# Expert down products of two tiles issued together, their 64-row remainders on the two row halves of TensorE's array

## The chip, the cores and the metric

The kernel runs on one core of a Trainium2 chip. Its engines are TensorE (PE; its weight loads are shown apart as PEld), VectorE (DVE), ScalarE (ACT), GpSimd (POOL) and SyncE (SP), which work at the same time and are ordered only by semaphores. The metric is the device time of one execution in microseconds (us); less is better. Before the change the median of three runs is 740.0 us (739.35 to 742.32).

## The reference

1024 tokens of width 256 pass through two layers, each an attention block and a mixture of experts, each with layer norms around it and a residual. Only the routed experts matter here. Cut to them:

```python
# layer 0: every token goes to its top 4 of 32 experts, inner width I = 192
g = silu(einsum('th,eih->tei', xf, gate_w)); u = einsum('th,eih->tei', xf, up_w)
routed = einsum('tei,ehi,te->th', g * u, down_w, combine)
# layer 1: the same with inner width F = 176 and at most 128 tokens for an expert
g = einsum('ech,ehf->ecf', buf, w_gate); u = einsum('ech,ehf->ecf', buf, w_up)
y = einsum('ecf,efh->ech', silu(g) * u, w_down)
```

All of this is in fp32.

## The kernel before

The routed work is sorted by expert and cut into tiles of at most 128 rows: 63 in layer 0 (`NTILE[0]`; the last of them may be empty, which depends on the routing) and 32 in layer 1. Tiles have a running number `g` over both layers (`E0` is 0 and 63) and a number `i` in their layer. A tile goes through these stages:

- **SP** loads the expert's weights, 512 KB into a ring of eight slots (`w_ex`) and the last 64 rows of the down weights into `w_rest`, where an even `g` takes partitions 0 to 63 and an odd one partitions 64 to 127. A slot is loaded again when `e_down` says that the tile eight before is done (lines 634 to 649).
- **POOL** gathers 128 token rows with an indirect DMA (layer 0 has 32 such row tiles, layer 1 has 32), and later scatters a tile's result rows to DRAM (`rows_to_outs`, line 812, in order of tiles).
- **PE, ups** (`e_up`, line 1185): gate and up products. The inner width of 192 (176) is 128 plus a remainder of 64; so there are three 128-column blocks by two halves of the contraction, 6 matmuls of 128x128 by 128 columns. An fp32 matmul is two weight loads and two matmuls in the trace, so they are 12 entries of line 1196. Rows are turned by PE ahead of that (`e_transpose`, line 1167), one row tile a step until all 32 are turned (after step 28).
- **ACT** (`e_silu`, lines 1486 and 1488) and **DVE** (`e_mult`, lines 2102 and 2106): silu and product. The remainder's product goes to the 64 rows of `eact` that belong to the parity of `g`; the other 64 rows are zeros that POOL wrote once per layer (line 800).
- **PE, down** (`e_down`, line 1201): 128 rows of the inner width by 256 columns (line 1209), then the remainder (line 1211) with all 128 rows of `w_rest`, half of which meets the zeros. Each is two entries of the trace. The result stands in PSUM bank 6 or 7, by the parity of `g`.
- **DVE** (`e_out`, line 2109) copies the bank to SBUF. Before a down may write its bank, PE waits for `e_sb` to reach `g - 1` (line 1206): the tile two before, in the same bank, has been copied out.

The order on PE is written out: step `i` gives out the transposes, the ups of tile `i`, and then the down of tile `i - 3` (`LAG` is 3, line 1242). The order on DVE is written out as well and is not touched by the change: step `i` is `e_mult(i)` and then `e_out(i - 3)` (line 2117). ACT's is `e_tile` (copy of turned rows) and `e_silu(i)`.

Behind the loop, the four choices of each token are summed from DRAM: SP loads four planes of 1 MB each (line 673), DVE adds them (line 2137). In layer 0 the loads wait until every tile that has rows is written; in layer 1 plane `k` waits for the tiles up to `28 + k`. In layer 1 PE has four products of the shared expert to do behind the loop (line 1132).

Elsewhere in the kernel PE uses a part of the array: in attention `weigh` (line 1014) issues four fp32 matmuls with 32 weight columns each, one for each quarter of the columns of the array; lines 1143 and 1175 use 32 of its rows.

Of the kernel before, what the change touches and what calls it, by code (L numbers as in the profile page):

```python
# [14 lines left out]
P = 128  # L15
T = 1024
NT = T // P
D = 256
KD = D // P
# [33 lines left out]
HALF = P // 2  # L53
FULL = 1
SFULL = tuple(w // P for w in SHARED)
UPC = 2 * FULL + 1
EW = KD * UPC * P + D
# [3 lines left out]
NTILE = (NROWT + E - 1, E)  # L61
E0 = (0, NTILE[0])
NR = (E, E + 1)
RING = 4
ROW_RING = 8
# [3 lines left out]
LAG = RING - 1  # L69
# [22 lines left out]
def turn_before(i):  # L92

    return min(2 * i + 1, i + LAG)


def copy_before(i):

    return min(2 * i + 1, i + LAG)


GATES_AT = D
# [192 lines left out]
def build(nc, a, out):  # L295
    ctx = ExitStack()
    with ctx:
        sems = {}

        def S(name):  # L300
            if name not in sems:
                sems[name] = ctx.enter_context(nc.semaphore(name))
            return sems[name]
# [120 lines left out]
        eact = X[:, 2048:3072].rearrange("p (r n) -> p r n", r=RING)  # L424
# [9 lines left out]
        w_ex = KAf[:, 0:ROW_RING * EW].rearrange("p (r n) -> p r n", r=ROW_RING)  # L434
        w_rest = X[:, 6144:6144 + ROW_RING // 2 * D].rearrange("p (r n) -> p r n", r=ROW_RING // 2)
# [69 lines left out]
        ps = ctx.enter_context(nc.psum_tensor("ps", [P, 8, CH], F32))  # L505
# [177 lines left out]
        def _(pool):  # L683
# [58 lines left out]
            for L in range(2):  # L742
# [52 lines left out]
                    pool.wait_ge(S("zero_rest"), 1)  # L795
                pool.memset(acts[L][HALF:P, f * T:(f + 1) * T], 0.0).then_inc(S("zero_rest"), 1)
                pool.memset(w_sdn[HALF:P, f, :], 0.0).then_inc(S("zero_rest"), 1)
                for x in range(2):
                    no = HALF * (1 - x)
                    pool.memset(eact[no:no + HALF, x::2, P:2 * P], 0.0).then_inc(S("zero_rest"), 1)  # L800

                def rows_in(i):
                    g = NROWT * L + i
# [53 lines left out]
        def _(pe):  # L857
# [19 lines left out]
            for L in range(2):  # L877
# [21 lines left out]
                for i in range(NT):  # L899
                    pe.wait_ge(S(f"qk_sb{L}"), i // 2 + 1)  # L900
                    dst = ps[:, qk_bank(L, i // 2), i % 2 * D:(i % 2 + 1) * D]
                    for k in range(KD):
                        mm = pe.matmul(dst, xT[:, k, i * P:(i + 1) * P], w_qkv[:, 2, k, :],
                                       start=(k == 0), stop=(k == KD - 1))
# [132 lines left out]
                def shared_up(u, those=(0, 1), ks=range(KD)):  # L1037
                    n, j = divmod(u, nsc)
                    q = UP_POS[L][u]
                    if L == 1 and q >= 2:  # L1040
                        pe.wait_ge(S(f"s_act{L}"), q - 1)
                    those = those if j < SFULL[L] else those[:1]
                    for x in those:
                        col = (x * SFULL[L] + j if j < SFULL[L] else 2 * SFULL[L]) * P
                        for k in ks:
                            mm = pe.matmul(ps[:, up_bank(L, u, x), :], w_sgu[:, k, col:col + P],  # L1046
                                           xT[:, k, n * CH:(n + 1) * CH], start=(k == 0), stop=(k == KD - 1))
                    if (those[-1] == 1 or j == SFULL[L]) and ks[-1] == KD - 1:
                        mm.then_inc(S("s_gu"), 1)
# [30 lines left out]
                if L == 0:  # L1080

                    for j in range(NT):
                        mm = pe.matmul(ps[0:E, LISTS, 0:1], picked[:, j, :], ones[:, 0:1], start=(j == 0), stop=(j == NT - 1))
                    mm.then_inc(S("counts"), 1)

                for i in range(NT):
                    for j in range(i + 1):
                        mm = pe.matmul(ps[:, RANKS, i * E:(i + 1) * E], (ones if j < i else before)[:, :],
                                       picked[:, j, :], start=(j == 0), stop=(j == i))
                mm.then_inc(S(f"ranks{L}"), 1)  # L1090
                if L == 0:
# [9 lines left out]
                    for x in range(2):  # L1101
                        mm = pe.matmul(ps[0:E, LISTS, 2 * E + 1 + x:2 * E + 2 + x], upto_n[:, E * x:E * (x + 1)], ones[0:E, 0:1],
                                       start=True, stop=True)
# [3 lines left out]
                def list_tokens(quarters):  # L1107

                    wide = 2 * NROWT
                    parts = token_parts  # L1110
                    for q in quarters:
                        pe.wait_ge(S("token_hi"), NT * L + QT * (q + 1))
                        if L == 1 or q < QUARTERS - 1:
                            pe.wait_ge(S("token_lo"), (QUARTERS - 1) * L + q + 1)
                        pe.wait_ge(S("at_place"), QUARTERS * L + q + 1)
                        for i in range(QT * q, QT * (q + 1)):
                            for k in range(K):
                                mm = pe.matmul(ps[:, LISTS, 2 * P:2 * P + wide], at_place[:, i, k, :],
                                               parts[:, i, k, :, :].rearrange("p a n -> p (a n)"),
                                               start=(i == 0 and k == 0), stop=(i == NT - 1 and k == K - 1))  # L1120
                    if quarters[-1] == QUARTERS - 1:
                        mm.then_inc(S("token_ps"), 1)
# [3 lines left out]
                def shared_down(i):  # L1126
                    pe.wait_ge(S(f"s_act{L}"), nsc * (i // TPC + 1))
                    banks = (SHARED_EARLY, 2)[L]
                    if i >= banks:
                        pe.wait_ge(S("sh_sb"), NT * L + i - banks + 1)  # L1130
                    for j in range(nsc):
                        mm = pe.matmul(ps[:, shared_bank(L, i), 0:D], actv[:, j, i * P:(i + 1) * P], w_sdn[:, j, :],  # L1132
                                       start=(j == 0), stop=(j == nsc - 1))
                    mm.then_inc(S("sh_down"), 1)

                if L == 0:
                    pe.wait_ge(S("zero_rest"), 1 + 4)
                    for i in range(SHARED_EARLY):
                        shared_down(i)
                    list_tokens((0,))  # L1140
                    pe.wait_ge(S("seg_of"), 1)
                    pe.wait_ge(S("dest_done"), 1)
                    pe.matmul(ps[:, RANKS, 0:4 * TILES[0]], ones_f[0:E, :], seg_of.rearrange("p a n -> p (a n)"),
                              start=True, stop=True).then_inc(S("seg_ps"), 1)
                    list_tokens((1, 2, 3))
                    for i in range(SHARED_EARLY, NT):
                        shared_down(i)
                else:
                    for u in UP_ORDER[1][nsc:]:
                        shared_up(u)  # L1150
                        if u == LIST_AFTER:
                            list_tokens(range(QUARTERS))
                    pe.wait_ge(S("zero_rest"), 1 + 4 * 2)
                    for i in range(TPC):
                        if i < 2:
                            pe.wait_ge(S("s_act1"), nsc * NC - 2 + 2 * i)
                        shared_down(i)
# [40 lines left out]
                                           start=(k == 0), stop=(k == KD - 1))  # L1198
                    mm.then_inc(S("e_up"), 1)

                def e_down(i):
                    g = E0[L] + i
                    r = g % ROW_RING
                    pe.wait_ge(S("e_act"), 2 * g + 2)
                    if g >= 2:
                        pe.wait_ge(S("e_sb"), g - 1)
                    if g == 1:
                        pe.wait_ge(S("places"), 1)
                    pe.matmul(ps[:, 6 + g % 2, 0:D], eact[:, g % RING, 0:P], w_ex[:, r, KD * UPC * P:EW],  # L1209
                              start=True, stop=False)  # L1210
                    mm = pe.matmul(ps[:, 6 + g % 2, 0:D], eact[:, g % RING, P:2 * P], w_rest[:, r // 2, :],  # L1211
                                   start=False, stop=True)
                    mm.then_inc(S("e_down"), 1)

                pe.wait_ge(S("dest_done"), L + 1)
                pe.wait_ge(S(f"s_act{L}"), nsc * NC)
# [4 lines left out]
                def load_place(i):  # L1221

                    if L == 0 and i < NTILE[0]:
                        places_of[i] = pe.value_load(seg_at[0:1, i:i + 1], min_val=0, max_val=(NROWT - 1) * P)
# [3 lines left out]
                for i in range(NTILE[L] + LAG):  # L1228
                    if i < NTILE[L]:
                        load_place(i + 1)  # L1230
                        while turned_to <= min(turn_before(i), NROWT - 1):
                            e_transpose(turned_to)
                            turned_to += 1
                        if L == 0 and i == 2:
                            pe.wait_ge(S("sh_sb"), NT)
                        e_up(i)
                    if L == 0 and i < 2:
                        (turn_list, spread_list)[i]()
                    if L == 1 and i == LAG:
                        pe.wait_ge(S("sh_sb"), NT + TPC)  # L1240
                    if i >= LAG:
                        e_down(i - LAG)
                for i in range(TPC if L == 1 else NT, NT):
                    shared_down(i)
                if L == 0:
# [2 lines left out]
                for k in range(K):  # L1248
                    pe.wait_ge(S("gate_diag"), K * len(ON_PE[0]) * L + len(ON_PE[L]) * (k + 1))
                    for x, i in enumerate(ON_PE[L]):  # L1250
                        if x == 0 or k == K - 1:
                            pe.wait_ge(S(f"sum_in_{k}_{i // TPC if k == K - 1 else 0}"), 16 * (L + 1))
                        mm = pe.matmul(ps[:, 2 + x, 0:D], gate_diag(L, x, k), sums[L][k][:, i, :],
                                       start=(k == 0 and L == 1), stop=(k == K - 1))
# [1032 lines left out]
```

## Time and profile before

| | us |
|---|---|
| median of three runs | 740.0 |
| the profiled execution | 741.1 |
| its span from the first to the last instruction | 739.4 |
| PE matmul busy | 661.2 (89%) |
| PE weight load busy | 429.0 (58%) |
| DVE busy | 479.0 (65%) |
| ACT busy | 327.0 (44%) |
| POOL busy | 265.2 (36%) |
| expert loop of layer 0, first ups to last copy out | 221.0 to 373.4 |
| expert loop of layer 1 | 630.1 to 708.3 |

Busy shares are means over stages with different limits, so the rows below are taken from the two expert loops and what follows each. A PE matmul's entry starts when it is issued to the array and its end is modelled; the time from one start to the next is what tells the rate.

### The profile page before, as it was taken

To read this page: it belongs to the slowest core of one execution; us is meant where nothing else is said; L and a number is where in the kernel's file an instruction comes from. 1 tells how busy PE (TensorE), PEld (TensorE's weight loads), DVE (VectorE), ACT (ScalarE), POOL (GpSimd) and SP (SyncE) were. 2 spreads that over 40 slices of the span, in tenths; PEclk is the share of its full clock that TensorE was granted. 3 is DMA by queue.
4 is the path that set the end of the run, shared out by engine and by line. 5 is a ranking of instruction groups with operands and counts; after the bars stand their busy time and mean duration, and the time that the engine had idled before them with its cause. 6 is when DMAs were issued, how large, how long until landed. Compare 5 with 4: busy or idle time off the path is not lost. (4 is left out here: it accounts for less than half of the span.)

```text
span 739.4 us, 13365 instructions
## 1 busy us (share of the span) xinstructions
PE 661.2 (89%) x4292; PEld 429.0 (58%) x4292; DVE 479.0 (65%) x1357; ACT 327.0 (44%) x686; POOL 265.2 (36%) x313
## 2 busy tenths in 40 slices
PE   4988999998779999999966887999998999999991
PEld 3633343335358999999953523343344446999980
DVE  3688888864663446445476798888865685344457
ACT  3554666673153333224412443666664230433322
POOL 4150212111266776444431282112111203677631
PEclk9998999999799999999996989999999999999995
DMA  3534210070049999999670444011000710489762
GB/s 103 171 115 130 66 37 1 1 233 25 30 133 308 311 334 301 299 311 309 223 256 1 129 136 136 16 52 71 1 2 1 257 53 25 155 284 316 238 215 92
DMA packets 60295, 108.60 MB, mean 147 GB/s; under 512 B 11194, under 2 KB 37131, under 8 KB 60100
## 3 DMA queue, kind: packets, MB, share of 16 engines
q1 hardware_dynamic: 52532, 93.86, 39.0%
q0 software_dynamic: 7632, 13.86, 5.6%
q8 instruction: 36, 0.59, 0.3%
q14 instruction: 31, 0.25, 0.1%
q10 hardware_dynamic: 64, 0.03, 0.0%
HBM read 79.98 MB, written 19.79 MB: 135 GB/s over the span
## 5 line engine op out<-in xcount | busy, mean ns | idle before, releaser
L1364 ACT ACTIVATE X<-ps 128x1024 f32<-128x1024 f32 (+1 forms) x192 | 147.5, 810 | 81.9 <-PE ps L1000 81.3
L1690 DVE TENSOR_REDUCE mx<-ps 128x1 f32<-128x512 f32 (+3 forms) x208 | 129.5, 674 | 26.2 <-PE ps L932 17.1
L932 PE MATMUL ps<-KA,QA 112*128 112x512 bf16 (+3 forms) x384 | 117.8, 343 | 7.9 <-DVE mx L1690 3.3
L815 POOL DMA_INDIRECT outs<-w_sgu,token x95 | 95.4, 1004 | 74.7 <-DVE w_sgu L2115 59.6
L779 POOL TENSOR_SCALAR_AFFINE_SELECT X<-X 128x512 f32<-128x512 f32 x64 | 40.7, 637 | 203.7 <-ACT X L1364 203.7
L2102 DVE TENSOR_TENSOR X<-ps,X 128x128 f32<-128x128 f32 x95 | 27.6, 291 | 113.3 <-ACT X L1488 111.7
L1000 PE MATMUL ps<-QA,KA 114*128 114x512 bf16 (+3 forms) x384 | 95.6, 332 | 2.4 <-ACT X L1364 1.2
L1196 PE MATMUL ps<-QA,KA 128*128 x756 | 96.1, 277 | 0.8 <-issue 0.8
L1196 PEld LDWEIGHTS ps<-QA,KA 128*128 128x128 f32 x756 | 92.9, 193 | 3.6 <-issue 1.8
L932 PEld LDWEIGHTS ps<-KA,QA 112*128 112x128 bf16 x384 | 37.1, 98 | 86.2 <-DVE mx L1690 41.3
L807 POOL DMA_INDIRECT V<-token_rows,row_of_slot x64 | 65.6, 1025 | 53.8 <-DVE row_of_slot L2010 31.5
L1014 PE MATMUL ps<-X,V 128*32 128x512 f32 (+3 forms) x768 | 81.5, 500 | 0.6 <-POOL X L779 0.6
L1486 ACT ACTIVATE X<-ps 128x128 f32<-128x128 f32 x95 | 26.3, 277 | 109.0 <-PE ps L1196 108.0
L1687 DVE CUSTOM_DVE_ANT_0 xT<-ps,xT 128x384 bf16<-128x384 f32 (+1 forms) x96 | 56.7, 620 | 8.1 <-PE ps L932 7.1
L1046 PE MATMUL ps<-xT,w_sgu 128*128 128x512 f32 x112 | 55.0, 635 | 3.7 <-POOL rstd L731 2.2
L1000 PEld LDWEIGHTS ps<-QA,KA 114*128 114x128 bf16 x384 | 33.6, 99 | 41.5 <-ACT X L1364 16.5
L1209 PE MATMUL ps<-KA,X 128*128 128x256 f32 x190 | 56.9, 381 | 0.3
L1211 PE MATMUL ps<-X 128*128 128x256 f32 x190 | 56.5, 379 | 0.0
L1196 PE MATMUL ps<-X,KA 128*128 128x128 f32 x384 | 48.2, 275 | 0.3 <-ACT X L1477 0.3
L1196 PEld LDWEIGHTS ps<-X,KA 128*128 128x128 f32 x384 | 45.6, 192 | 0.6 <-ACT X L1477 0.5
L2115 DVE COPY w_sgu<-ps 128x256 f32<-128x256 f32 x95 | 40.3, 424 | 4.2 <-PE ps L1211 1.2
L1211 PEld LDWEIGHTS ps<-X 128*128 128x128 f32 x190 | 36.1, 190 | 4.9
(319 smaller groups left out, 891.0 us busy)
## 6 DMA issues: line engine op xcount, KB each, us to landing
KA<-in_ex SPq DMA_DIRECT2D x95, 512.0 KB
X<-in_dn SPq DMA_DIRECT2D x95, 64.0 KB
outs<-empty SPq DMA_DIRECT2D x4, 1024.0 KB, 8.0
V<-outs SPq DMA_DIRECT2D x4, 1024.0 KB, 6.1
QA<-X SPq DMA_DIRECT2D x28, 128.0 KB, 2.5
KA<-X SPq DMA_DIRECT2D x28, 128.0 KB, 2.6
QA<-w_sdn SPq DMA_DIRECT2D x28, 128.0 KB, 2.5
KA<-parts_k SPq DMA_DIRECT2D x28, 128.0 KB, 2.5
```

The costliest lines, as they stand in the source:

```text
L807: pool.indirect_dma_start(out=rows[:, g % ROW_RING, :], out_offset=None, in_=token_rows[L], in_offset=bass.IndirectOffsetOnAxis(ap=row_of_ ...
L815: pool.indirect_dma_start(out=outs[L], out_offset=bass.IndirectOffsetOnAxis(ap=token[L][:, i:i + 1], axis=0), in_=erows[:, g % OUT_RING, : ...
L932: mm = pe.matmul(ps[:, bank, j * w:(j + 1) * w], QA[0:KQ, h, i * P:(i + 1) * P], KA[0:KQ, h, s0:s0 + w], start=True, stop=not diag or mask ...
L1000: mm = pe.matmul(ps[:, 4 + 2 * p + x, off:CH], KA[0:KX, h, b * P:(b + 1) * P], QA[0:KX, h, c * CH + off:(c + 1) * CH], start=True, stop=True)
L1014: mm = pe.matmul(ps[32 * x:32 * x + 32, RB, off:CH], V[:, b, HG * g + x, :], probs[:, st % PB, x, off:CH], start=(b == 0), stop=(b == TPC ...
L1046: mm = pe.matmul(ps[:, up_bank(L, u, x), :], w_sgu[:, k, col:col + P], xT[:, k, n * CH:(n + 1) * CH], start=(k == 0), stop=(k == KD - 1))
L1196: mm = pe.matmul(ps[:, 2 + g % RING, m * P:(m + 1) * P], w_ex[:, r, col:col + P], rowsT_all[:, k, bass.ds(at, P)] if L == 0 else rowsT(L, ...
L1209: pe.matmul(ps[:, 6 + g % 2, 0:D], eact[:, g % RING, 0:P], w_ex[:, r, KD * UPC * P:EW], start=True, stop=False)
L1211: mm = pe.matmul(ps[:, 6 + g % 2, 0:D], eact[:, g % RING, P:2 * P], w_rest[:, r // 2, :], start=False, stop=True)
L1364: nc.scalar.activation(probs[:, st % PB, 2 * p:2 * p + 2, off:CH], ps[:, 4 + 2 * p:6 + 2 * p, off:CH], ACT.Exp, scale=SCALE).then_inc(S(f" ...
L1687: ins = v.tensor_tensor_reduce(mask_sums[:, u % 2, 0:w], ps[:, n % RB, 0:w], mask_wide[:, CH - w:CH], 1.0, -BIG, ALU.add, ALU.max, mx[:, p ...
L1690: ins = v.tensor_reduce(mx[:, part, i, h0:h0 + nh], ps[:, n % RB, 0:nh * w].rearrange("p (h w) -> p h w", h=nh), AX.X, ALU.max)
```

## The change

A step no longer gives out one down. `downs_after` says after which step which downs come: two at a time behind every second step, an even `g` and the odd one after it, and single ones at the ends (tile 62 of layer 0, tiles 0 and 31 of layer 1). `e_downs` gives out the 128-row parts of the two tiles first and then the two remainders, each with 64 rows of weights and 64 rows of data in place of 128. The zeros aren't written any more.

```diff
+def downs_after(L, i):
+
+    if i < NTILE[L]:
+        return tuple(x for x in (i - 3, i - 2) if x >= 0) if (E0[L] + i) % 2 else ()
+    return {NTILE[L]: (NTILE[L] - 3, NTILE[L] - 2), NTILE[L] + 1: (NTILE[L] - 1,)}.get(i, ())
...
-                for x in range(2):
-                    no = HALF * (1 - x)
-                    pool.memset(eact[no:no + HALF, x::2, P:2 * P], 0.0).then_inc(S("zero_rest"), 1)
...
-                def e_down(i):
-                    g = E0[L] + i
-                    r = g % ROW_RING
-                    pe.wait_ge(S("e_act"), 2 * g + 2)
-                    if g >= 2:
-                        pe.wait_ge(S("e_sb"), g - 1)
-                    if g == 1:
-                        pe.wait_ge(S("places"), 1)
-                    pe.matmul(ps[:, 6 + g % 2, 0:D], eact[:, g % RING, 0:P], w_ex[:, r, KD * UPC * P:EW],
-                              start=True, stop=False)
-                    mm = pe.matmul(ps[:, 6 + g % 2, 0:D], eact[:, g % RING, P:2 * P], w_rest[:, r // 2, :],
-                                   start=False, stop=True)
-                    mm.then_inc(S("e_down"), 1)
+                def e_downs(those):
+                    for i in those:
+                        g = E0[L] + i
+                        pe.wait_ge(S("e_act"), 2 * g + 2)
+                        if g >= 2:
+                            pe.wait_ge(S("e_sb"), g - 1)
+                        if g == 1:
+                            pe.wait_ge(S("places"), 1)
+                        pe.matmul(ps[:, 6 + g % 2, 0:D], eact[:, g % RING, 0:P], w_ex[:, g % ROW_RING, KD * UPC * P:EW],
+                                  start=True, stop=False)
+                    for i in those:
+                        g = E0[L] + i
+                        half = slice(HALF * (g % 2), HALF * (g % 2) + HALF)
+                        pe.matmul(ps[:, 6 + g % 2, 0:D], eact[half, g % RING, P:2 * P], w_rest[half, g % ROW_RING // 2, :],
+                                  start=False, stop=True).then_inc(S("e_down"), 1)
...
-                    if L == 1 and i == LAG:
+                    if L == 1 and i == LAG - 1:
                         pe.wait_ge(S("sh_sb"), NT + TPC)
-                    if i >= LAG:
-                        e_down(i - LAG)
+                    e_downs(downs_after(L, i))
```

The counts that PE waits for on `zero_rest` are lowered by the two writes that are gone.

## Rows read from the trace of the kernel before

**Rows 1.** Stretch of layer 0's loop: us, PE, PEld, DVE, ACT, POOL busy, clock, DMA

```profile
300.99:316.41 15.42, 15.42 (x114) 14.70 (x112) 7.07 (x22) 3.81 (x14) 6.88 (x8) 1.00 0.94 302
```

**Rows 2.** Chain that ended last, loop of layer 1: start, us, what

```profile
664.56 1.34 PE ps L1196 x12
...
666.98 1.34 PE ps L1196 x12
...
700.48 1.34 PE ps L1196 x12
...
702.25 0.43 PE ps L1211 x2
702.68 1.35 PE ps L1196 x12
```

**Rows 3.** Timeline, layer 0, ups of tile 32 and what follows them

```profile
300.99 1.50 PE L1196 MATMUL ps<-QA,KA 128*128 x12
...
302.52 0.28 ACT L1486 ACTIVATE X<-ps 128x128 f32<-128x128 f32 x1 [1.63 <-PE ps L1196]
...
303.12 0.29 DVE L2102 TENSOR_TENSOR X<-ps,X 128x128 f32<-128x128 f32 x1 [1.13 <-ACT X L1488]
...
303.77 0.42 DVE L2115 COPY w_sgu<-ps 128x256 f32<-128x256 f32 x1
```

**Rows 4.** Timeline, layer 0's last ups (tile 62) and the downs behind them

```profile
367.59 1.50 PE L1196 MATMUL ps<-QA,KA 128*128 x12
...
370.38 0.91 DVE L2115 COPY w_sgu<-ps 128x256 f32<-128x256 f32 x2
370.92 0.30 PEld L1209 LDWEIGHTS ps<-KA,X 128*128 128x128 f32 x2 [0.50 <-issue]
...
371.45 0.59 PE L1211 MATMUL ps<-X 128*128 128x256 f32 x2
```

**Rows 5.** Timelines and one line's durations: attention's column-quarter matmuls between full ones

```profile
520.66 0.38 PE L932 MATMUL ps<-KA,QA 112*128 112x512 bf16 x1
520.97 1.07 PE L1014 MATMUL ps<-X,V 128*32 128x512 f32 x8
...
521.96 0.10 PEld L932 LDWEIGHTS ps<-KA,QA 112*128 112x128 bf16 x1 [0.84 <-issue]
...
L1014 PE MATMUL ps<-X,V x8: 592/604/617, 521.0 to 521.4; 128*32 128x512 f32 x8
```

**Rows 6.** Durations ns (min/median/max) of matmuls just behind a switch of array shape

```profile
L1143 PE MATMUL ps<-X x2: 374/426/478, 210.1 to 210.4; 32*128 32x256 f32 x2
...
L1046 PE MATMUL ps<-xT,w_sgu x3: 592/595/697, 567.4 to 568.8; 128*128 128x512 f32 x3
...
L1167 PE MATMUL ps<-identf,V x2: 273/301/329, 222.6 to 222.8; 128*128 128x128 f32 x2
```

**Rows 7.** Timelines, end of layer 0's loop: a scatter, plane load, plane add

```profile
364.97 0.98 POOL L815 DMA_INDIRECT outs<-w_sgu,token  x1 [1.23 <-DVE w_sgu L2115]
...
366.71 0.40 SPq L673 DMA_DIRECT2D V<-outs  x1
...
379.46 1.67 DVE L2137 SCALAR_TENSOR_TENSOR X<-V,xn,X 128x256 f32<-128x256 f32 x4 [1.62 <-DMA V<-outs]
```

**Rows 8.** Timeline, layer 0, DVE's steps 48 and 50

```profile
340.11 0.29 DVE L2102 TENSOR_TENSOR X<-ps,X 128x128 f32<-128x128 f32 x1 [2.35 <-ACT X L1488]
...
343.94 0.19 DVE L1917 TENSOR_REDUCE gsum<-gate 128x8 f32<-128x32 f32 x1
...
344.83 0.42 DVE L2115 COPY w_sgu<-ps 128x256 f32<-128x256 f32 x1
```

**Rows 9.** Chain that ended last, end of layer 1's loop

```profile
707.79 2.12 DMA outs<-w_sgu,token
...
709.95 7.80 DMA X<-outs
```

**Rows 10.** Timeline, POOL's first instruction behind the zeros of layer 0

```profile
201.91 0.17 POOL L825 CAST X<-X 32x1 f32<-32x1 int32 x1 [10.44 <-DVE X L1948]
```

More of the change, by code:

```diff
@@ L1136, in _ @@
                 if L == 0:
-                    pe.wait_ge(S("zero_rest"), 1 + 4)
+                    pe.wait_ge(S("zero_rest"), 1 + 2)
                     for i in range(SHARED_EARLY):
@@ L1152, in _ @@
                             list_tokens(range(QUARTERS))
-                    pe.wait_ge(S("zero_rest"), 1 + 4 * 2)
+                    pe.wait_ge(S("zero_rest"), 1 + 2 * 2)
                     for i in range(TPC):
```

## The prediction

> **What bounds the kernel now.** I read the stretches of the two expert loops first, then the chain of waits, then the timeline. In a stretch of seven steps of layer 0, PE is busy all of its 15.42 us at a granted clock of 1.00 (the 2.4 GHz level), while DVE is busy 7.07 us, POOL 6.88 us and the DMA engines 0.94 of the time [rows 1]. The chain runs over PE alone: ups 1.34 us, down parts 0.43 us each, and the next ups [rows 2]. A step is 2.20 us where nothing is turned (700.48 to 702.68) and 2.42 us where a row tile is (664.56 to 666.98), so transposes are 0.22. PE sets the pace, and the change works on PE.
>
> All times below count from the start U of a tile's ups. Within a step the ups are 1.34, the 128-row part 0.43 and the remainder 0.43. After the ups comes a chain on other engines: silu begins at U+1.53, the product at U+2.13, and DVE's copy of the down three tiles back runs from U+2.78 to U+3.20 [rows 3]. That copy stands behind the product in DVE's order, and the change leaves this order alone.
>
> **Part 1, the remainders.** Before, two tiles' remainders are four passes of 0.215 us, 0.86 in all [rows 2]. If the halves run side by side they are two, 0.43. Whether passes of separate parts of the array do that is not shown for 64 rows. The nearest rows are the column quarters: eight fp32 passes of 512 columns, each 0.43 at the rate of the 128-row part, start from 520.97 to 521.4 and the next full weight load begins at 521.96, 0.99 us later instead of 3.4 [rows 5]. I take side by side, a gain of 0.43 a pair. The other ends are no overlap (gain 0) and overlap of one pass only (0.215).
>
> **Part 2, the switches of shape.** Each pair goes from the full array to halves and back. Going in, 512 bf16 columns that start at 520.66 have streamed by 520.87 (512 at 2.4 GHz), and the first quarter begins at 520.97: 0.10. Coming back, 0.99 less two rounds of 0.43 and the first quarters' own load (617 against 592 ns) leaves 0.10 [rows 5]. In a plain stream the loads are hidden. Behind a switch the first one isn't: a matmul behind quarters takes 697 ns against 592, so 0.105 for 128 fp32 columns; with 32 rows and 128 columns it is 478 against 374, the same; transposes pay 329 against 273, 0.055 [rows 6]. So a pair pays 0.10 + 0.105 going in and 0.10 + 0.105 (0.055 before transposes) coming back: 0.41 or 0.36. Part 1's 0.43 is eaten but for 0.02 or 0.07 us a pair. If the loads of the two halves follow one another, 0.105 more.
>
> The Trainium skill speaks against the change here: "TensorEngine Tiling (Array Packing)", Key Properties, says that a change of tiling mode, and not merely of the tile, drains TensorE. The rows above agree for quarters and for 32 rows with 0.10 us each way; without that rule the sum would be the second rival's.
>
> **Part 3, the wait that comes new.** The second down of a pair needs the bank of the tile two before it. At PE's step i the pair is tiles i-3 and i-2, and DVE copies tile i-4 out in its step i-1, behind the product of tile i-1. That ends 3.20 behind the start U of the ups of tile i-1 [rows 3]. Before, PE had two steps of slack on this. Now only the ups of tile i and one 128-row part lie between: 1.34 + 1.34 + 0.43 puts the second part at U+3.10, or U+3.32 with 0.22 of transposes. The trace of before holds this very wait, at the loop's end, where three downs follow without ups. The copy of tile 59 ends near 370.8, the weight load waits until 370.92, and the remainder starts at 371.45, so the 128-row part streamed from 371.45 - 0.43 = 371.02, which is U+3.43 [rows 4]. So the second part starts at U+3.43: late by 0.33 without transposes, by 0.10 with them. Behind the wait stands all of PE's stream, the remainders and the next ups too.
>
> **A pair of steps.** Without transposes: 3.43, second part until 3.86, switch 0.205, remainders 0.44, switch 0.205: the ups of tile i+1 start at U+4.70, against 4.41 before. **+0.29.** With them: 3.86 + 0.205 + 0.44 + 0.155 + 0.22 = 4.88 against 4.85, **+0.025** with unrounded terms. DVE's work of a pair, twice 1.07 us, fits, and weight slots come free no later than before by more than 0.1 us, so the DMA's 0.94 doesn't become the bound when the period grows.
>
> **Layer 0.** What ends the layer is the load of the planes: SP's load waits until 367.1, for the scatter that POOL issued at 364.97, tile 56's (the seventh from the last; the tiles behind it hold no rows), and at 379.46 DVE waits 1.62 us for a plane [rows 7]. So I sum up to the copy of tile 56. Twelve pairs with transposes (steps 5 to 27) give 0.3, the first pair, which waits for no bank, -0.1, and fifteen without (steps 29 to 57) 15 x 0.29 = 4.4. In step 50 DVE has 0.89 us of gate work ahead of the copy [rows 8]; that goes into the wait of the pair behind step 51: 0.9. At tile 48 ACT takes an exponential in, and DVE waits 2.35 for it where 1.13 is usual [rows 3, 8]; of these 1.2 us I count 0.1, as the downs of a pair that then lie between the ups of tiles 47 and 48 give ACT 4.70 - 1.34 - 2.20 = 1.16 us more. Tile 56 itself is copied 0.6 later within its pair, since its remainder comes behind its partner's 128-row part, the wait and the switch. Sum 6.2. The last copy (tile 62) moves by more, some 8.3, since its three downs now wait for one another; DVE's adds begin behind it, at 381.7 instead of 373.4, but the third plane lands at 379.4 + 6.2 = 385.6, when two adds of 1.67 are done. So **+6.2**.
>
> **Layer 1.** Tile 0 alone pays two switches with nothing to share, 0.35. Twelve pairs with transposes 0.3, the one behind step 28 0.1, the one behind step 30 0.3, and one more down stands ahead of the last ups, 0.87: the ups of tile 31 end 1.9 later. Behind them, tile 28's copy is where it was; tile 29's comes after its partner's wait, and its scatter follows it at U+5.9 instead of U+5.3: 0.6. Plane 1 waits for that scatter [rows 9]. Planes 0 and 1 start 1.9 and 2.5 later; I take **+2.3**. The shared expert's four products on PE start 3.3 later, but their last consumer waits for plane 1 ahead of them.
>
> **Nothing** comes from the zeros: POOL wrote them ahead of 10.44 us in which it waits for DVE [rows 10]. Without that cover it would be a gain of their own length.
>
> **Sum:** 6.2 + 2.3 = 8.5 us. On the profiled execution's 741.1 (span 739.4 and 1.7 around it) that is 749.6; the median of before is 1.1 less, so **748.5**.
>
> **Rivals.**
> *The halves don't share the array in time.* For it: a remainder's two passes are issued one behind the other, so a strict order would overlap only the first tile's second pass with the second tile's first. Against it: the quarters are issued in the same way and took two rounds. Price: 44 pairs on the path, 44 x 0.215 = 9.5, so 758; with no overlap at all 767. With the two loads in series 44 x 0.105 = 4.6: 753. The Trainium skill, "TensorE: Matmul & The Clock Gate", Part 3, has matmuls start and end strictly in program order, which would give the 758; the quarters' 0.99 us speaks against it.
>
> *The halves need no switch* (faster than before). No row shows a 64-row shape. If a half's weights load behind full matmuls, a pair is 3.86 + 0.44 = 4.30 without transposes (-0.11) and 4.52 with them (-0.33). Layer 0: 15 x -0.11, 12 x -0.33, first pair -0.4, gates and tile 48 1.0, tile 56's place 0.4: -4.7. Layer 1: 12 x -0.33, two more pairs -0.4, one down 0.9, its end 0.4: -3.1. That is 732. It decides from a switch price below 0.1 a pair or so, where the bank wait alone is left.
>
> *The bank is free in time.* If the copy came before the product, pairs would be -0.03 and -0.08: layer 0 -1.3, layer 1 +0.5, 739. Against it: DVE's written order and [rows 4].
>
> **How the numbers follow.** Forecast 0.64 (746 to 751); loads in series 0.08 (753); passes in order 0.12 (758, or 767); no switch 0.06 (732); bank in time 0.10 (739). The range leaves out the no-switch case, half of the last and the longest of the serial case: 741 to 759. A measurement of this kernel tells about 0.5% (3.7 us) from no change. Faster by more is the no-switch case, 0.06; within it the bank case, 0.10; the rest, 0.84, is slower.
>
> **What would show it.** In the changed trace: the 64-row matmuls of line 1211's successor start in twos within some 10 ns, the pair 0.43 and not 0.86; the weight load ahead of them begins 0.10 behind the last full column and the one after them too; in each pair a PE gap before the second 128-row part, 0.33 without transposes, ending just behind DVE's copy; ups 4.70 apart over two steps late in layer 0. I am wrong if the two-step period is 4.41 or less there, if line 1209's second part never waits, or if layer 0's planes start less than 4 us later.

## The result and the profile after

The changed kernel takes 751.1 us (median of four runs, 747.6 to 754.4) against 741.0 (739.4 to 742.3): the ratio of the two is 1.0129, 95% interval 1.0102 to 1.0157, so the change is slower, clear of noise, by less than 2%. Ratios here and below come from runs taken side by side, with runs in a slower state left out, and so are not quite the quotient of the medians. The forecast was 748.5 with a range of 741 to 759, and slower. The profiled execution took 753.05 us with a span of 751.3, 11.9 above the 739.4 of before.

In the changed code the ups stand on line 1200, the 128-row parts on 1213, the 64-row remainders on 1218, DVE's copy on 2120, the planes' loads on 680. The first rows are the chain of waits of the changed kernel in layer 0, late, where nothing is turned (start, us, what; they answer [rows 2]).

```profile
361.00 2.88 PE ps L1200 x24
363.88 0.43 PE ps L1213 x2
364.39 0.67 PE ps L1213 x2
365.06 0.63 PE ps L1218 x4
365.69 2.88 PE ps L1200 x24
```

A pair is 4.69 us (361.00 to 365.69) where two steps were 4.41. The first 128-row part has streamed by 364.31, the second ends at 365.06 and so began at 364.63: 0.32 of waiting, for DVE's copy. Four 64-row passes and the switch ahead of them take 0.63. The four start in twos, 7 ns apart within each two, the second two 0.32 us behind the first. The rows are the first two of the pair at 365.06, then all four, with durations and the first and last start:

```profile
L1218 PE MATMUL ps<-X x2: 480/480/480, 365.0 to 365.0; 64*128 64x256 f32 x2
...
L1218 PE MATMUL ps<-X x4: 376/428/480, 365.0 to 365.3; 64*128 64x256 f32 x4
```

In layer 1's chain a pair with transposes is 4.86 us:

```profile
699.94 0.97 PE ps L1213 x4
...
704.80 0.97 PE ps L1213 x4
```

The loop is as forecast. The ends of the two layers are not. The same chain at layer 0's end, then at layer 1's:

```profile
381.05 0.63 PE ps L1218 x2
381.67 1.92 PE ps L1252 x8
383.60 5.63 PE ps L1258 x26
389.25 0.88 DVE stats L2186 x2
...
711.10 1.55 PE ps L1200 x12
...
718.73 12.61 PE ps L1136 x48
```

Where layer 0 ends, PE now runs without a pause from the last remainder through its twenty products for the sum of the planes (lines 1252 and 1258, 40 entries in the trace, of which the chain names 34), and DVE waits for these. Where layer 1 ends, the chain of before ran over a scatter and a plane's load [rows 9]; now it runs over the four products of the shared expert (line 1136), which took 12.61 us. The windows of that stretch show why (PE, PEld, DVE, ACT, POOL busy, clock, DMA):

```profile
712.40:715.40 3.00, 1.58 (x9) 0.86 (x9) 1.01 (x3) 2.36 (x5) 1.19 (x2) 1.00 0.11 44
715.40:718.40 3.00, 2.40 (x8) 1.00 (x4) 1.66 (x5) 1.21 (x5) 1.71 (x3) 0.60 0.11 44
718.40:721.40 3.00, 3.00 (x8) 2.20 (x8) 0.42 (x1) 1.24 (x5) 1.96 (x2) 0.50 0.81 243
```

PE was busy for 1.58 of 3 us, the downs waiting for one another's copies, and then the granted clock stood at 0.50 (the 1.2 GHz level).

So the 11.9 us of span are: 0.9 that lie ahead of the loop (tile 3's ups start at 231.20 instead of 230.29; no down has been given out by then, and the start of the first ups differs by up to 4.8 us between the profiles of this case), 5.8 in layer 0 (the first product of the attention that follows starts 6.7 later, less the 0.9), 0.1 between the layers, 1.8 in layer 1's loop, 3.3 behind its last ups.

### The profile page after: what moved, and what is told of

Same layout as the page of the kernel before. It is cut to its first block, busy times and chain, and to the rows that moved or that the text cites. A ratio compares the mean times of both kernels' runs of the same rounds, so it can differ in the third digit from the quotient of the medians.

```text
span 751.3 us, 13361 instructions
## 1 busy us (share of the span) xinstructions
PE 669.3 (89%) x4292; PEld 406.2 (54%) x4292; DVE 478.4 (64%) x1357; ACT 326.9 (44%) x686; POOL 263.1 (35%) x309
## 4 chain that ended last, share of the span: by engine, by line
PE 72%; DVE 19%; issue 3%; ACT 2%; DMA 2%; POOL 1%; SPq 1%; ACTq 0%; DVEq 0%; POOLq 0%
PE ps L1200 17%; PE ps L1018 9%; PE ps L936 8%; PE ps L1004 7%; PE ps L1213 6%; DVE mx L1695 5%; PE ps L1050 4%; PE ps L1218 4%; PE ps L1136 3%; PE ps L1171 2%; PE ps L891 2%; PE ps L990 1%; DVE xres L1600 1%; PE ps L969 1%; PE ps L907 1%
## 5 line engine op out<-in xcount | busy, mean ns | idle before, releaser
L1200 PEld LDWEIGHTS ps<-QA,KA 128*128 128x128 f32 x756 | 89.0, 194 | 7.1 <-issue 7.0
L811 POOL DMA_INDIRECT V<-token_rows,row_of_slot x64 | 65.6, 1026 | 57.2 <-DVE row_of_slot L2015 32.1
L1050 PE MATMUL ps<-xT,w_sgu 128*128 128x512 f32 x112 | 53.2, 618 | 3.7 <-POOL rstd L738 2.2
L1213 PEld LDWEIGHTS ps<-KA,X 128*128 128x128 f32 x190 | 28.9, 191 | 20.5 <-issue 16.3
L738 POOL TENSOR_TENSOR rstd<-rs_sq,minus_half 128x4 f32<-128x4 f32 (+1 forms) x14 | 13.6, 969 | 63.1 <-DVE rs_sq L1557 63.1
```

What stands on the lines that cost most here:

```text
L811: pool.indirect_dma_start(out=rows[:, g % ROW_RING, :], out_offset=None, in_=token_rows[L], in_offset=bass.IndirectOffsetOnAxis(ap=row_of_ ...
L1200: mm = pe.matmul(ps[:, 2 + g % RING, m * P:(m + 1) * P], w_ex[:, r, col:col + P], rowsT_all[:, k, bass.ds(at, P)] if L == 0 else rowsT(L, ...
```

## The experiments

The times stand against the kernel before as run beside them on the same chip: 741.95 us for the order without the halves, the halves without the order, the copies a step sooner and the whole product at layer 1's end; 742.66 for the copy-first kernel with its loads spread and the groups of four with rows loaded tile by tile, both forms; 741.77 for the other four.

**The order without the halves.** Zeros and full remainders come back, the pairs stay.

```diff
+                for x in range(2):
+                    no = HALF * (1 - x)
+                    pool.memset(eact[no:no + HALF, x::2, P:2 * P], 0.0).then_inc(S("zero_rest"), 1)
...
-                        pe.matmul(ps[:, 6 + g % 2, 0:D], eact[half, g % RING, P:2 * P], w_rest[half, g % ROW_RING // 2, :],
+                        pe.matmul(ps[:, 6 + g % 2, 0:D], eact[:, g % RING, P:2 * P], w_rest[:, g % ROW_RING // 2, :],
```

> The pairs' order alone: the remainders are full 128-row products again, over zeros in the unused half, so nothing shares the array and no shape is switched. Theory (the new wait for the bank costs the time, halves and switches cancel): a pair of steps late in layer 0 is 3.43 + 0.43 + 0.86 = 4.72 us without transposes (changed kernel 4.69, before 4.41) and 3.43 + 0.43 + 0.86 + 0.22 = 4.94 with them (4.87, 4.85); the whole is 0 to 3 us above the changed kernel, 751 to 754. Rival (the switches of shape cost it, not the order): pairs back at 4.41 and 4.85, the whole at 741.

750.3 us (ratio 1.0117, 1.0072 to 1.0162), as the changed kernel. Its chain in layer 0 (its ups on line 1203, remainders on 1220):

```profile
361.43 2.68 PE ps L1203 x24
364.11 0.43 PE ps L1216 x2
...
364.62 0.67 PE ps L1216 x2
365.29 0.86 PE ps L1220 x4
366.16 2.68 PE ps L1203 x24
```

A pair is 4.73, the wait for the bank is there unchanged, the remainders take 0.86 and no switch stands around them (2.68 for 24 ups instead of 2.88). So the order alone costs what the change costs, and halves with their switches give 0.04 a pair.

**The halves without the order.** One down a step as before, its remainder on its half.

```diff
 def downs_after(L, i):
-    if i < NTILE[L]:
-        return tuple(x for x in (i - 3, i - 2) if x >= 0) if (E0[L] + i) % 2 else ()
-    return {NTILE[L]: (NTILE[L] - 3, NTILE[L] - 2), NTILE[L] + 1: (NTILE[L] - 1,)}.get(i, ())
+    return (i - 3,) if i >= 3 else ()
```

> The halves alone: the order of the kernel before, one down in every step, with its 64-row remainder on its half, so that each tile switches into the halves and back and nothing shares the array. Theory (a switch in and out costs 0.41 us, 0.36 ahead of transposes): a step late in layer 0 goes from 2.20 to 2.61 us, one with transposes from 2.42 to 2.78; with some 30 steps of the one kind on the path of layer 0 and 7 in layer 1, and 29 and 25 of the other, 37 x 0.41 + 54 x 0.36 = 35 us more than before, 776. Rival (halves need no drain of the array, the row-tiled products load their weights behind full ones as any other): steps stay at 2.20 and 2.42, the whole at 741. Between them (only the exposed load of 0.105 each way): 2.41 and 2.58, 758.

771.5 us (1.0403, 1.0357 to 1.0449), 29.5 more than before where 35 were expected; that a step costs 0.02 less than priced makes some 2 of the difference; the rest has not been taken apart. Its chain in layer 0:

```profile
363.13 1.53 PE ps L1198 x12
364.67 0.43 PE ps L1211 x2
365.10 0.63 PE ps L1216 x2
365.73 1.53 PE ps L1198 x12
```

A step is 2.60 us instead of 2.20 [rows 2], with transposes 2.77 instead of 2.42: a switch in and out costs 0.39 and 0.35. And two 64-row passes take 0.63 here, as long as the four of two tiles in the changed kernel. The halves run side by side.

**DVE copies a step sooner.** Both tiles of a pair are copied behind the pair, ahead of the next product.

```diff
-                    if i >= LAG:
-                        e_out(i - LAG)
+                    for x in downs_after(L, i):
+                        e_out(x)
```

> The changed kernel, but DVE copies both downs of a pair out right behind the product of the same step, one step sooner, so that the bank is free when the next pair wants it. Theory (the bank wait is the cost): no gap ahead of the second 128-row part, a pair is 2.68 + 0.86 + 0.205 + 0.43 + 0.205 = 4.38 us without transposes and 2.68 + 0.22 + 0.86 + 0.205 + 0.43 + 0.155 = 4.55 to 4.80 with them (before 4.41 and 4.85), the whole is 738 to 742. Rival 1 (PE is late for another reason, the switches or the loads): the gap stays or moves behind the remainders, pairs at 4.69, the whole at 751. Rival 2 (DVE becomes the bound, since the two copies now wait for PE ahead of the next product): gaps ahead of the 128-row parts that end on DVE's product, a pair above 4.5.

736.4 us (0.9930, 0.9904 to 0.9956): faster than the changed kernel by 2% and than the kernel before by 0.7%, which is clear of noise. Its timelines of PE and then of DVE in layer 0:

```profile
303.26 2.94 PE L1200 MATMUL ps<-QA,KA 128*128 x24
306.04 1.03 PE L1213 MATMUL ps<-KA,X 128*128 128x256 f32 x4
307.00 0.70 PE L1218 MATMUL ps<-X 64*128 64x256 f32 x4
307.63 1.60 PE L1200 MATMUL ps<-QA,KA 128*128 x12
...
303.36 0.76 DVE L2120 COPY w_sgu<-ps 128x256 f32<-128x256 f32 x2 [0.27 <-PE ps L1218]
```

The two 128-row parts are one piece, the gap is gone, a pair is 4.37 us. With transposes it is 4.77, and step 51, where the gates had put 0.89 into the wait, is a step as any. One change of order, on an engine that is idle half of the time [rows 1], was worth some 15 us of the changed kernel. So the wait for the bank is the cost: it goes with the copy's place, and it is there without halves.

**Layer 1's end, filled with a whole product.** One of the shared expert's four products moves between the last pair's 128-row parts, one ahead of the last down.

```diff
                                   start=True, stop=False)
+                        if L == 1 and i == NTILE[1] - 3:
+                            shared_down(TPC)
...
+                    if L == 1 and i == NTILE[1] + 1:
+                        shared_down(TPC + 1)
                     e_downs(downs_after(L, i))
...
```

> The changed kernel, with two of the shared expert's four last products of layer 1 moved up between the last downs, where PE waits for DVE's copies. Theory (PE's idle gaps there let the granted clock fall to 0.50 from 716 to 723 us, which stretches the four products from 10.5 to 12.7 us): the clock stays at 1.00 behind the last ups, the last product ends 3 to 4 us sooner and the whole is 1 to 4 us below the changed kernel, 747 to 750. Rival (the end of layer 1 hangs on the scatter of tile 29 and the planes' loads, not on PE): planes land when they did, the whole within 0.5 us of the changed kernel.

752.1 us (1.0167, 1.0117 to 1.0216), no gain: the rival's number, though the planes did not land when they did before. The clock held at 1.00 and the last product's last matmul began at 726.1 instead of 731.0, but the chain went elsewhere:

```profile
717.46 5.47 DMA outs<-w_sgu,token
...
722.95 5.29 DMA X<-outs
```

A product is 2.6 us long where the gap was 1.42, so tile 29's copy came later and its scatter went out at 717.46, behind plane 0's load of 717.03; it took 5.47 us where it took 2.12 before [rows 9], and plane 1's load waits for it (722.95, against 720.79 in the changed kernel, whose last ups are 0.5 later).

**The same, with half a product.** Three of the product's six chunks in the gap, three ahead of the last down.

```diff
+                        if L == 1 and i == NTILE[1] - 3:
+                            shared_down(TPC, (0, 3))
...
+                    if L == 1 and i == NTILE[1] + 1:
+                        shared_down(TPC, (3, nsc))
...
```

> The changed kernel, with the first half of one of the shared expert's products put into PE's wait of 1.4 us between the last pair's 128-row parts, and its second half ahead of the last down, so that neither down moves by more than some 0.2 us. Theory (the clock that fell to 0.50 behind these waits cost 2 to 3 us at the end): the clock stays at 1.00 until the four products are done, these end 4 us sooner than 730.95, the scatter of tile 29 goes out where it did, and from the last ups to the end takes 32 to 33 us in place of 35.4: 748 to 749. Rival (planes and their loads set the end, as they did where a whole product stood between the parts): products sooner, end within 1 us of the changed kernel, 750 to 752.

748.5 us (1.0094, 1.0058 to 1.0131), where the changed kernel took 752.0 on the same chip. Windows and chain of the stretch:

```profile
712.20:715.20 3.00, 3.00 (x15) 1.86 (x13) 1.66 (x5) 1.16 (x4) 1.74 (x2) 1.00 0.11 44
715.20:718.20 3.00, 3.00 (x14) 2.67 (x15) 1.01 (x3) 1.28 (x5) 1.97 (x2) 1.00 0.88 244
...
713.86 3.91 DMA outs<-w_sgu,token
...
717.79 5.45 DMA X<-outs
```

PE has no gap, the clock stays at 1.00, the scatter goes out ahead of plane 0's load (714.37), and the chain runs over scatter and plane again as it did before the change. From the start of the last ups' last matmul to the start of the last output add it is 32.0 us (709.20 to 741.23) instead of 35.4 (712.36 to 747.74), and it was 32.1 before the change: the 3.3 us are back. This run moves work as well as holding the clock, so it doesn't part the two. The pairs with full remainders do, in the main: they have the same first wait of 1.42 us and no work moved, their clock stayed at 1.00, and there it is 32.6 us (711.99 to 744.55), over a scatter and a plane too. So 2.8 of the 3.3 go with the clock; their second wait is shorter, 0.18 instead of 0.60, so up to some 0.4 of that can be the wait itself.

**The changed kernel once more.**

> The changed kernel once more, as a measure of how its end varies. If the fall of the clock at 716 us belongs to the gaps that the change makes there, it is there again, with some 35 us from the last ups to the end; if it is chance, the clock is 1.00 there and the end takes 32 to 33 us, as in the kernels that also have those gaps. 748 to 753.

752.0 us (750.1 to 755.2). Layer 1's end is the same again (35.5 us, clock 0.64 and then 0.50), in both executions of this kernel that were profiled, and in neither of the two whose gaps were filled. So the fall goes with the gaps and is not the chance of one execution, though the pairs with full remainders, with nearly the same waits, did not have it. In this execution the clock also fell at layer 0's end, where it stayed at 1.00 in the first. Its window there and its first eight matmuls of the planes' sum, which took 1.99 us in the other:

```profile
380.00:383.00 3.00, 3.00 (x8) 2.02 (x7) 2.33 (x6) 0.00 (x0) 2.21 (x3) 0.50 1.09 383
...
380.53 3.78 PE L1252 MATMUL ps<-X,identf 128*128 128x256 f32 x8
```

The three last downs of layer 0 wait for one another as well, 1.42 and 0.60 us in both executions. From the last ups of layer 0 to the first of layer 1 it is 2.4 us longer with the fall (263.0 instead of 260.6). A fall that comes in some executions only fits the spread of 747.6 to 755.2 over the changed kernel's eight runs, but which of them had it is not known beyond the two profiled.

**Who releases layer 0's planes.** In the kernel before, SP's eight register loads, which stand between its last weights' load and the planes' loads, are spread over its last eight weights' loads.

```diff
+                    if L == 0 and REGS_AT <= i < REGS_AT + OUT_RING:
+                        x = i - REGS_AT
+                        those.append(sp.value_load(used_rows[0:1, x:x + 1], min_val=16,
+                                                   max_val=16 * uses(NTILE[0] - 1, OUT_RING)))
...
```

> The kernel before, with SP's eight loads of registers (some 0.55 us each) that stand between the last weights' load of layer 0 and the planes' loads spread over its last eight weights' loads. Theory (SP's own queue releases the planes' loads, not a scatter): the first plane's load goes out 3.5 to 4.5 us sooner than 366.71, at 362.2 to 363.2, DVE no longer waits 1.62 us for the third plane, and the layer ends up to 1.5 us sooner: 739 to 741. Rival (the scatter of the seventh tile from the end, which POOL issued at 364.97, releases them): 366.7 as before, the whole unchanged.

741.1 us (0.9981, 0.9961 to 1.0000). SP's timeline and, from 374.26, the chain:

```profile
362.85 0.48 SPq L607 DMA_DIRECT2D X<-in_dn  x1
363.65 0.40 SPq L678 DMA_DIRECT2D V<-outs  x1
...
374.26 0.43 PE ps L1216 x2
374.69 1.73 PE ps L1252 x8
376.42 5.63 PE ps L1258 x26
```

The planes' loads follow the last weights' load by 0.8 us. Against the last ups they go out 4.8 us sooner than before (6.9 ahead of 370.59, where it was 2.1 ahead of 368.82), the layer's last adds come 2.2 us sooner, and the chain then runs over PE's products. The releaser was SP's own queue. The time is at the edge of what can be told from no change.

**The same in the copy-first kernel.**

> The copy-first kernel with SP's eight register loads of layer 0's end spread over the last weights' loads. The kernel before gained 2.2 us from this between its last ups and the last add of layer 0, and 0.7 in the median. Theory (the same wait stands in the copy-first kernel, which ends that layer 13.3 us behind its last ups): 1 to 2 us less than 736.4, 734 to 736. Rival (DVE's last copy sets the start of the adds, as in the changed kernel, where the planes are there by then): 736 to 737.

738.6 us (0.9945, 0.9920 to 0.9969), the copy-first kernel's time within the intervals: the rival's number. Its chain there runs from the last remainder into PE's planes' products, as in the changed kernel:

```profile
371.54 0.63 PE ps L1223 x2
372.17 1.92 PE ps L1257 x8
374.09 5.62 PE ps L1263 x26
```

In the copy-first kernel itself the planes were not all there: DVE waited for the third, as the theory had it.

```profile
374.34 1.67 DVE L2142 SCALAR_TENSOR_TENSOR X<-V,xn,X 128x256 f32<-128x256 f32 x4 [1.06 <-DMA V<-outs]
```

With the loads spread that wait is gone, but the layer's last add starts only 0.3 us sooner behind the last ups (12.6 us, 12.9 before), since PE's products for the planes now end last.

**Groups of four.** One switch for four tiles, behind every fourth tile's ups: two 128-row parts, four remainders, two 128-row parts, their results in the two halves of the two banks. DVE copies all four behind the group.

```diff
+                    for i in firsts:
+                        part(i, True)
                     for i in those:
...
+                        mm = pe.matmul(ps[:, 6 + g % 2, out_at(g)], eact[half, g % RING, P:2 * P],
+                                       w_rest[half, g % ROW_RING // 2, :], start=i in lasts, stop=i in firsts)
...
+                    for i in lasts:
+                        part(i, False).then_inc(S("e_down"), 1)
```

> Groups of four downs behind every fourth tile's ups, in the order: two 128-row parts, four 64-row remainders (two side by side, twice), two 128-row parts; their results in the two halves of the two banks; DVE copies all four out behind the group. One switch into the halves and back then serves four tiles in place of two. Theory (the halves' gain is eaten by the switch, 0.40 us measured without and 0.345 with transposes): four steps are 4 x 1.34 + 4 x 0.43 + 2 x 0.43 + 0.40 = 8.34 us without transposes (two pairs of the copy-first kernel 8.75, before 8.81) and 4 x 1.56 + 1.72 + 0.86 + 0.345 = 9.17 with them (9.53, 9.70); 15 groups in layer 0 and 7 in layer 1 save 15 x 0.38 + 7 x 0.36 = 8 us of the copy-first kernel's 736.4: 728. Rival 1 (the weights' loads become the bound: the DMA engines are busy for 0.94 of 8.81, 8.28 us in four steps, and four slots now come free together): gaps ahead of the ups that end on DMA, four steps at 8.5 to 8.8, 732 to 736. Rival 2 (DVE's four copies behind one another hold up its products): gaps ahead of the group that end on DVE, four steps above 8.8, 737 or more.

757.9 us (1.0203, 1.0140 to 1.0266). The group itself is as priced: from the first part at 312.02 to the next ups at 315.01 it is 2.99 us (1.72 + 0.86 + 0.40 = 2.98). But PE waits ahead of the ups behind which the next group stands; the second row is a window of layer 0's loop:

```profile
310.58 1.60 PE L1213 MATMUL ps<-QA,KA 128*128 x12 [1.55 <-issue]
...
306.03:316.35 10.32, 8.77 (x68) 7.72 (x68) 3.92 (x14) 2.19 (x8) 3.94 (x4) 1.00 0.84 275
```

Four steps take 10.2 us, PE is busy for 0.85 of the time and the DMA engines for 0.84. The profile names no releaser for that wait ("issue"). The first rival fits it, far beyond its price of 8.8: four slots come free in one burst, and the loads of a tile's remainder rows stand behind those of its pair's second tile. The next run tests this.

**Groups of four, remainder rows loaded tile by tile.**

```diff
                     expert_in(g, e)
-                    if g % 2 == 0 and i + 1 < NTILE[L]:
-                        return e
-                    if g % 2 == 1 and i > 0:
-                        rest_in(g - 1, even)
-                    elif i >= ROW_RING:
-                        sp.wait_ge(S("e_down"), g - ROW_RING + 2)
                     rest_in(g, e)
```

> The groups of four, with each tile's 64 remainder rows of down weights loaded right behind its own other weights, in place of both remainders of a pair behind the second tile's (with halves a tile no longer reads its partner's rows, so it need not wait for them). Theory (in the groups of four, four steps took 10.19 us without transposes as PE waits 1.55 us for weights whose loads wait for each other; DMA's work in four steps is 0.82 to 0.85 of 10.19, 8.4 us): the first tile of a burst is there some 2 us sooner, the gap ahead of the ups closes, four steps take 8.4 to 8.8 us, the whole 728 to 738. Rival (four slots that come free together leave the queue empty whatever the order): a gap of over 1 us stays, four steps at 9.5 or more, the whole at 748 or more.

740.1 us (0.9963, 0.9933 to 0.9993). A window of four steps without transposes, and the longest wait that the trace names for PE between the ups of tiles 9 and 53:

```profile
303.37:311.74 8.37, 8.37 (x66) 7.52 (x65) 3.76 (x12) 2.18 (x8) 3.93 (x4) 1.00 0.99 331
...
290.39 0.44 PE L1178 MATMUL ps<-identf,V 128*128 128x128 f32 x2 [1.35 <-DMA V<-token_rows,row_of_slot]
```

The gaps of over 1 us ahead of the ups are gone, so the order of the loads had made them. PE has its 8.37 where the loads keep up, and the DMA engines are at 0.99 there. Other groups lose this again: between the ups of tiles 9 and 53 the loop takes 100.0 us here and 99.95 in the copy-first kernel. The waits that the trace names there end on the gathers of token rows, ahead of three transposes (0.42, 0.41 and 1.35 us); elsewhere in that stretch four steps without transposes take up to 8.72 us, with no wait named. That the DMA work as a whole bounds this loop fits, but isn't shown. Either way PE's gain of 0.4 us in four steps did not show in the loop's time. The whole is no better than the copy-first kernel; why it is not equal to it has not been taken apart. The same with SP's register loads spread:

> Groups of four with the remainders' rows loaded tile by tile, and SP's register loads spread. If the gap ahead of the ups closes in the one, 1 to 2 us less than it, as a best version: 727 to 736. The register loads, 0.55 us each, lie between weights' loads from tile 55 on; if the weights are the bound there, they cost up to 8 x 0.55 = 4.4 us and it is slower than the one without by that much.

738.9 us (0.9972, 0.9947 to 0.9997): no measurable difference from the one without. None of the variants measured faster than the copy-first kernel.

## Why the prediction was right, and where not

**Part 1 held.** Side by side was the choice between 0, 0.215 and 0.43. Two tiles' four passes take the 0.63 of one tile's two with its switch, so the gain is 0.43. The rule of a strict order in the Trainium skill's "TensorE: Matmul & The Clock Gate", Part 3, taken pass by pass, would have given 758; the trace, with starts in twos, doesn't bear that reading out for row halves, as it didn't for column quarters. (The price of that rival counts 44 pairs; the terms of the forecast hold 28 and 14. That is 0.4 us.)

**Part 2 held.** 0.41 and 0.36 a pair were the terms; 0.39 and 0.35 were measured. That quarters and 32-row shapes were the nearest rows for a 64-row shape [rows 5, 6] was good enough to 0.02 us. For 32 rows those rows show a first load left uncovered and no drain; the 0.10 each way rests on the quarters alone. The Trainium skill's sentence that a change of tiling mode drains TensorE ("TensorEngine Tiling (Array Packing)", Key Properties) agrees with the 0.39 of the halves alone.

**Part 3 held to 0.02 us a pair.** The wait that [rows 4] showed in the loop's end is the one that stands in every pair: 0.32 for a forecast of 0.33; pairs 4.69 and 4.86 for 4.70 and 4.88. Tile 56's copy, up to which the terms were summed, moved by 5.7 for 6.2 (without the 0.9 ahead of the loop). The gates' 0.89 are in the trace of the changed kernel at step 51, DVE's last gate work and its copy, and PE's wait for that:

```profile
349.51 0.19 DVE L1926 TENSOR_TENSOR xn<-gate,gsum 128x32 f32<-128x32 f32 x1
349.74 0.42 DVE L2120 COPY w_sgu<-ps 128x256 f32<-128x256 f32 x1
...
350.31 0.67 PE L1213 MATMUL ps<-KA,X 128*128 128x256 f32 x2 [0.97 <-DVE w_sgu L2120]
```

The period of that pair is 0.89 longer than its neighbours'.

**Layer 0: the number held (6.2, measured 5.8), the reason did not.** "What ends the layer is the load of the planes", released by tile 56's scatter, was the step that failed. 0.40 at the load [rows 7] was time of issuing, not of waiting, and the eight register loads in SP's queue, which that row doesn't show, had been overlooked; the run that spread them showed that they set the time of the load. The first load moved from 366.71 to 371.68, by 4.1 us without the 0.9 ahead of the loop, not by 6.2. And the layer then ended on PE: its products for the planes begin behind the last down, which moved by more than the planes did (the last copy by 7.9 without the 0.9, forecast 8.3), and the planes, for which DVE still waited 1.62 us before [rows 7], are there by then. That the end moved by 5.8, close to the 6.2, is luck: the planes came 2.1 us sooner than forecast, and PE's products, which had no term, made up for it.

**Layer 1: the loop held, its end was mis-sized.** Ups 1.9 later were forecast, 1.8 were measured. Behind them 0.4 was the term and 3.3 the measurement. The prediction had seen that the last downs wait for each other, and that the shared expert's products start 3.3 us later but have a consumer that waits for plane 1 anyway. It had no term for the clock. With the gaps it fell, the products became 12.6 us long instead of 10.5, and that consumer had nothing else left to wait for. The half product in the gap gave the 3.3 us back, and where the clock stayed at 1.00 with no work moved, 2.8 of them were not there. With the 3.3 in place of the 0.4 the sum would have been 8.5 + 2.9 = 11.4, against 11.0 measured from the loop's start on.

**The rivals.** Passes in order and no switch are out by the numbers above. The bank in time had its mechanism and, with the copies moved, its pairs (4.37 and 4.77 for 4.38 and 4.77), but was not what the changed kernel does. Its price was 0.8 us below the kernel before (layer 0 -1.3, layer 1 +0.5); 5.5 were measured in the medians and 4.1 in the spans of the two profiles. Of these, 2.6 lie between the first and the last ups of layer 0 and 0.9 behind the last ups of layer 1; why has not been taken apart.

## What to carry to other kernels

When work of an engine is put together in larger pieces, go through the rings that it shares with others and ask for each which copy, load or slot now comes free a step too late. Here the halves of the array were worth 0.04 us a pair and the place of one copy in another engine's order 0.3. And gaps in PE's work can have a second price, its clock, which here fell due in the stretch behind them.

## What the runs showed of the hardware

Not expected was how little idle time precedes a fall of the clock: waits of 1.42 and 0.60 us between downs of some 0.6 to 1.2 us, and then 0.50 for some 7 us (0.60, 0.50 and 0.76 in three windows of 3 us from 715.4 on), although PE was at work without a gap from 717.5 on. The pairs with full remainders have the same first wait and a shorter second one, and there the clock stayed at 1.00 (its products took 10.52 us):

```profile
714.12 0.67 PE L1216 MATMUL ps<-KA,X 128*128 128x256 f32 x2 [1.42 <-DVE w_sgu L2122]
715.83 0.67 PE L1216 MATMUL ps<-KA,X 128*128 128x256 f32 x2 [0.18 <-DVE w_sgu L2122]
```

What decides between the two, and why the clock fell at layer 0's end in one execution and not in the other, no run here tells.

A scatter of one tile took 5.47 us when it went out 0.43 us behind a plane's load of 1 MB. It took 3.91 us when it went out 0.51 ahead of it, 2.44 when 0.71 ahead (the pairs with full remainders), and 2.12 when 1.12 ahead (before the change).
